# Second layer's experts: rows stored by an indirect scatter in token and choice order, last combination read with plain loads

## The chip, the cores and the metric

One core of one Trainium2 chip runs the whole program in one launch. The metric is device time in microseconds (us): the median of the runs of the kernel before is 1483.16 us (3 runs, 1478.87 to 1484.14).

## The reference, cut to what matters

Two layers of gated attention-like mixing and mixture-of-experts feed-forward work on 2048 tokens of 256 floats (batch 2, sequence 1024). What the change touches is the last part, the experts of the second layer:

```python
scores = sigmoid(x @ gate_w.T)                      # 2048 tokens x 32 experts
_, topk_ids = top_k(scores + e_bias, 4)             # four experts for each token
topk_w = take_along_axis(scores, topk_ids, axis=1)
topk_w = topk_w / sum(topk_w, axis=1, keepdims=True)
...                                                 # out[t] = sum over the 4 experts e of
                                                    #   topk_w * (silu(x w1[e]) * (x w3[e])) w2[e]
x = x + tanh(g_ffn[1]) * out
```

All of it is in float32, and the hidden width of an expert is 192.

## The kernel before, in words

The program is a row of stages. Each stage is a block in which every engine has its own instruction stream; at the end of a block each engine runs a drain instruction and then a barrier holds all engines until the last has arrived (the profile books the drain and the barrier on the line of the `with nc.Block()` or on a line near it). The last three stages are these.

`route` (layer 1) turns the router's scores into tables. Every token has four choices, which makes 8192 rows; they are sorted by expert and padded to tiles of 128 rows, 95 tiles in all (`NT1`). For each of the 95 x 128 places the stage must know which token stands there. It finds this with 64 small matmuls of one-hot matrices, which all add into one PSUM bank; the result is the token number plus one, or zero where a place is padding. VectorE turns it into `token_u`, the list of tokens by tile (lines 821 to 827), and also keeps `slot_u`, the place that each token's k-th choice was given (line 794).

`experts1` runs over the 95 tiles with rings of four buffers. For one tile: VectorE copies one column of `token_u` into `tcol` (line 897); GpSimd starts an indirect gather that fetches the 128 token rows from `xn1` in DRAM (`move_tiles`, line 864); TensorE transposes them (line 1045), multiplies by `w1` and `w3` of the tile's expert (line 1051), transposes the hidden rows (line 1057) and multiplies by `w2` (line 1066); ScalarE does the silu and two copies out of PSUM; VectorE does the product (line 1139) and copies the result to `ysb` (line 1127). SyncE stores `ysb` as a plain tile of 128 rows of 1 KB in tile order into `y1` (line 1156). Tiles overlap: VectorE, in its turn for tile j, copies out tile j-2 and makes the column for tile j+5; TensorE transposes the rows of tile j+2. The program's order on each engine is fixed, with a loop of four tiles per turn (`tile_loop`). The first layer's `experts0` has the same form but stores by an indirect scatter from GpSimd (line 875), into token and choice order, seven calls or so behind the gathers (`LAG`).

`combine` (layer 1) takes 16 tiles of 128 tokens. For each, GpSimd issues four indirect gathers (one for each choice, line 1201) that fetch the rows from `y1` by `slot_u` into a ring of four tiles. VectorE first computes the four weights of each token (lines 1214 to 1222) and then adds the four weighted rows to `x` (line 1233, 64 operations); ScalarE's queue stores each finished tile to the output (line 1247). VectorE and ScalarE run this in loops with register arithmetic. The first layer's combination has no gathers: SyncE loads each tile of 128 tokens with one plain transfer (line 1187).

## Time and profile before

| what | value |
|---|---|
| runs, median (lowest to highest) | 1483.16 us (1478.87 to 1484.14) |
| span of the profiled execution, first to last instruction | 1482.6 us |
| PE, DVE, ACT, POOL busy share of the span | 80%, 51%, 40%, 22% |
| gathers of `experts1` and `experts0` (line 864) | 134 of 952 ns |
| gathers of the last combination (line 1201) | 64 of 971 ns |
| mean DMA rate over the span | 78 GB/s |

The profile gives no time of the profiled execution beyond its span; the span lies 0.6 us under the median of the runs. The engines are PE (TensorE), DVE (VectorE), ACT (ScalarE), POOL (GpSimd) and SP (SyncE). A line with "q" after the engine, as in POOLq, is an instruction of that engine's sequencer (a wait, a register operation, a drain, or the issue of a transfer). All start times are microseconds from the start of the span.

### The profile page before, as it was taken

How to read it: one execution, taken by the hardware profiler on the slowest of the kernel's cores; microseconds unless marked ns; L12 is line 12 of the kernel's file. 1: busy time of each engine (PE TensorE's matmuls, PEld its weight loads, DVE VectorE, ACT ScalarE, POOL GpSimd, SP SyncE). 2: the span in 40 equal slices, each digit the busy share in tenths (PEclk: the TensorE clock that was granted, in tenths of full speed). 3: DMA queues.
4: the chain of work that ended last, by engine and by line, in shares of the span. 5: the costliest groups of instructions: out<-in, count | busy, mean ns of one | idle time of the engine just before them, and what ended most of it. 6: DMA issues, size and time to landing. Idle time of an engine off the chain costs nothing. (4 is left out here: it accounts for less than half of the span.)

```text
span 1482.6 us, 24652 instructions
## 1 busy us (share of the span) xinstructions
PE 1186.0 (80%) x5790; PEld 661.9 (45%) x5792; DVE 751.7 (51%) x2017; ACT 592.7 (40%) x1307; POOL 320.0 (22%) x527
## 2 busy tenths in 40 slices
PE   3485999999992587999999999998717999999200
PEld 1374667677672341233323323323614777777100
DVE  4334333333334467788888878851484333333432
ACT  2342111111110440677767767776425333333000
POOL 2001222222220602010110111100002333333564
PEclk9965999999996795899999999999756999999655
DMA  9710011011012774330330231202801333334343
GB/s 311 282 57 15 27 35 35 28 35 35 28 28 96 232 223 78 38 46 2 46 46 15 31 46 17 29 2 68 213 11 50 102 100 103 99 100 99 91 116 96
DMA packets 86256, 115.39 MB, mean 78 GB/s; under 512 B 14902, under 2 KB 71120, under 8 KB 86058
## 3 DMA queue, kind: packets, MB, share of 16 engines
q1 hardware_dynamic: 69594, 71.24, 19.0%
q0 software_dynamic: 14288, 41.30, 9.7%
q10 hardware_dynamic: 2304, 2.10, 0.4%
q8 instruction: 22, 0.36, 0.1%
q14 instruction: 48, 0.39, 0.1%
HBM read 84.01 MB, written 30.38 MB: 77 GB/s over the span
## 5 line engine op out<-in xcount | busy, mean ns | idle before, releaser
L1868 DVE TENSOR_REDUCE arena<-ps 128x1 f32<-128x512 f32 x512 | 327.9, 682 | 73.8 <-PE ps L1709 66.9
L1839 ACT ACTIVATE arena<-ps 128x512 f32<-128x512 f32 (+1 forms) x576 | 304.4, 598 | 143.0 <-PE ps L1750 141.8
L1750 PE MATMUL ps<-arena 99*128 99x512 bf16 (+1 forms) x576 | 218.0, 391 | 5.9 <-ACT arena L1839 5.6
L864 POOL DMA_INDIRECT xg<-xn,tcol x134 | 127.6, 952 | 433.0 <-DVE tcol L897 431.5
L1709 PE MATMUL ps<-arena 96*128 96x512 bf16 x512 | 207.0, 407 | 13.6 <-DMA arena<-k_parts 11.2
L1739 PE MATMUL ps<-arena 128*17 128x512 f32 (+1 forms) x1152 | 154.2, 607 | 2.1 <-ACT arena L1839 1.0
L967 ACT ACTIVATE scratch<-ps 128x512 f32<-128x512 f32 x78 | 46.6, 598 | 249.8 <-PE ps L942 249.8
L942 PE MATMUL ps<-arena,scratch 128*128 x312 | 142.4, 599 | 0.7 <-ACT scratch L962 0.6
L934 PE MATMUL ps<-arena,scratch 128*128 x624 | 141.2, 379 | 0.7 <-DVE scratch L999 0.7
L1051 PE MATMUL ps<-arena,scratch 128*128 x380 | 140.0, 491 | 0.2 <-issue 0.2
L1750 PEld LDWEIGHTS ps<-arena 99*128 99x128 bf16 (+1 forms) x576 | 57.2, 102 | 180.7 <-ACT arena L1839 138.9
L934 PEld LDWEIGHTS ps<-arena,scratch 128*128 128x128 f32 x624 | 115.6, 190 | 15.5 <-issue 1.4
L984 DVE TENSOR_TENSOR ysb<-ps,arena 128x256 f32<-128x256 f32 x39 | 16.6, 425 | 179.3 <-PE ps L934 179.3
L1139 DVE TENSOR_TENSOR scratch<-ps,scratch 128x192 f32<-128x192 f32 x95 | 34.0, 357 | 131.1 <-ACT scratch L1108 103.1
L1066 PE MATMUL ps<-arena,scratch 96*128 x380 | 97.8, 380 | 0.4 <-DVE ysb L1127 0.4
L999 DVE TENSOR_SCALAR scratch<-ps,arena 128x128 f32<-128x128 f32 x312 | 84.2, 343 | 26.6 <-PE ps L951 26.6
L942 PEld LDWEIGHTS ps<-arena,scratch 128*128 128x128 f32 x312 | 56.9, 193 | 58.4 <-issue 58.4
L1709 PEld LDWEIGHTS ps<-arena 96*128 96x128 bf16 x512 | 51.6, 101 | 62.2 <-DVE arena L1868 25.4
L1051 PEld LDWEIGHTS ps<-arena,scratch 128*128 128x128 f32 x380 | 65.4, 192 | 26.3 <-issue 1.5
L1658 POOL TENSOR_TENSOR scratch<-arena 128x64 f32 (+1 forms) x64 | 18.8, 294 | 265.7 <-DVE arena L1887 251.5
L1201 POOL DMA_INDIRECT arena<-y,slot_u x64 | 62.1, 971 | 40.6 <-issue 19.3
L1066 PEld LDWEIGHTS ps<-arena,scratch 96*128 96x128 f32 x380 | 64.5, 190 | 6.0 <-issue 0.9
(289 smaller groups left out, 1366.1 us busy)
## 6 DMA issues: line engine op xcount, KB each, us to landing
arena<-in_L_ffn_W SPq DMA_DIRECT2D x16, 1024.0 KB, 12.8
y<-ysb SPq DMA_DIRECT2D x95, 128.0 KB
arena<-in_L_ffn_w POOLq DMA_DIRECT2D x26, 384.0 KB, 10.1
arena<-in_L_ffn_w SPq DMA_DIRECT2D x44, 192.0 KB, 6.6
arena<-k_parts SPq DMA_DIRECT2D x48, 137.6 KB, 5.0
arena<-q_parts SPq DMA_DIRECT2D x96, 64.0 KB, 5.0
xn<-scratch SPq DMA_DIRECT2D x32, 128.0 KB, 1.7
scratch<-y SPq DMA_DIRECT2D x16, 256.0 KB, 2.8
```

What stands on the lines that cost most here:

```text
L864: pool.indirect_dma_start(out=e.xg[:, r, :], out_offset=None, in_=e.xn[layer], in_offset=bass.IndirectOffsetOnAxis(ap=e.tcol[:, r:r + 1], ...
L934: last = nc.tensor.matmul(ps[:, YB, 0:D], hT[:, k, :], e.w2[:, ex, k, :], start=(k == 0), stop=(k == HK0 - 1))
L942: ins = nc.tensor.matmul(ps[:, HB0 + n, :], xT[:, k, :], e.w1[:, ex, k, n * HB:(n + 1) * HB], start=(k == 0), stop=(k == DK - 1))
L999: v.tensor_scalar(hT[:, k, :], ps[:, TB + k // HALF, (k % HALF) * P:(k % HALF + 1) * P], e.b1T[:, bass.ds(ex * HK0 + k, 1)], 0.0, ALU.add, ...
L1051: ins = nc.tensor.matmul(ps[:, GB + r % 2, 0:2 * I1], xT[:, r % 2, k, :], e.w13[:, ex, k, :], start=(k == 0), stop=(k == DK - 1))
L1066: last = nc.tensor.matmul(ps[:, YB + r % 2, 0:D], aT[0:IH, r % 2, k, :], e.w2b[0:IH, ex, k, :], start=(k == 0), stop=(k == 1))
L1201: pool.indirect_dma_start(out=yg[:, u, k, :], out_offset=None, in_=e.y[1], in_offset=bass.IndirectOffsetOnAxis(ap=e.slot_u[:, i, k:k + 1], ...
L1709: nc.tensor.matmul(ps[:, MAXB + pos % NMAXB, :], e.q_aug[u][0:QROWS, c, h, t * P:(t + 1) * P], e.k_aug[u][0:QROWS, h, CL + k * HB:CL + (k ...
L1739: ins = nc.tensor.matmul(ps[h * 32:h * 32 + HD + 1, AB, :], e.v_g[u][0:rows, mt, h, :], e.prob[s % 2][0:rows, h, :], start=(mt == 0), stop ...
L1750: nc.tensor.matmul(ps[0:rows, SB + n % NSB, :], e.k_aug[u][0:AROWS, h, k0:k0 + rows], e.q_aug[u][0:AROWS, c, h, :], start=True, stop=True) ...
L1839: nc.scalar.activation(e.prob[s % 2][0:rows, h, :], ps[0:rows, SB + (s * GH + h) % NSB, :], ACT.Exp).then_inc(p_ready, 1)
L1868: v.tensor_reduce(e.mx[:, c, h, t, k:k + 1], ps[:, MAXB + pos % NMAXB, :], AX.X, ALU.max).then_inc(max_done, 1)
```

## The change

Four things change.

1. `route`, layer 1: the 64 matmuls now add into four PSUM banks, one for each choice, so that the choice of each place is known too. VectorE works out of them `row_u`, the destination row 4 x token + choice (or a spare row past the end for padding), in some nine operations more; `slot_u` is gone.
2. `experts1`: the plain store on SyncE is gone. GpSimd issues an indirect scatter per tile into `y1` instead, behind its gathers; VectorE copies one more column per tile (`rcol`). At the end GpSimd waits for the last scatters.
3. The four weights of each token are computed by VectorE at the start of `experts1`, after the first four columns.
4. The last combination has no indirect gathers and no ring: SyncE issues 16 plain loads of 512 KB, each 4 KB in one piece per partition, into 16 separate buffers, with no wait between them. VectorE's 64 operations and ScalarE's 16 stores are the same but written out, without a loop.

```diff
@@ make_env
-    e.slot_u = sb("slot_u", [P, NTILE, K1], U32)
-    e.y = [dram("y0", [NTOK * K0 + P, D]), dram("y1", [NT1 * P, D])]
+    e.y = [dram("y0", [NTOK * K0 + P, D]), dram("y1", [NTOK * K1 + RING1 * P, D])]
@@ route, VectorE, layer 1
-            ch(v.tensor_scalar(row_i, row, -1.0, None, ALU.add))
-            v.tensor_scalar(e.token_u[:, 0:nt].bitcast(I32), row_i, NTOK - 1, None, ALU.bitwise_and)
+                ch(v.tensor_reduce(row, ps[:, RB:RB + kk, 0:nt].rearrange("p k n -> p n k"), AX.X, ALU.add))
+                for k in range(1, kk - 1):
+                    v.tensor_scalar(late[k - 1], ps[:, RB + k, 0:nt], 0.0, float(k), ALU.is_gt, ALU.mult)
+                ch(v.tensor_scalar(row_i, row, -1.0, None, ALU.add))
+                v.tensor_scalar(e.token_u[:, 0:nt].bitcast(I32), row_i, NTOK - 1, None, ALU.bitwise_and)
+                v.scalar_tensor_tensor(none, row, 0.0, flat(spares)[:, 0:nt], ALU.is_equal, ALU.mult)
+                ch(v.tensor_scalar(late[kk - 2], ps[:, RB + kk - 1, 0:nt], 0.0, float(kk - 1), ALU.is_gt, ALU.mult))
+                v.scalar_tensor_tensor(row, row, float(kk), late[0], ALU.mult, ALU.add)
+                ch(v.tensor_tensor(late[1], late[1], late[2], ALU.add))
+                ch(v.scalar_tensor_tensor(none, none, -float(kk), row, ALU.add, ALU.add))
+                v.tensor_tensor(e.row_u[:, 0:nt], none, late[1], ALU.add)
@@ move_tiles
-    LAG = 2 + ring
+    LAG = (2 + ring, 3 + ring)[layer]
...
-            if layer == 1 or (isinstance(j, int) and j < 0):
+            if isinstance(j, int) and j < 0:
                 return
             pool.wait_ge(y_ready, j + 1)
             pool.sem_inc(carrier, 1)
...
+        for r, stored in enumerate(y_stored):
+            pool.wait_ge(stored, 16 * ((nt - 1 - r) // len(y_stored) + 1))
@@ experts1, VectorE
                 if at_least(j, RING1):
                     dve.wait_ge(y_stored[r], turn * 16)
+                v.tensor_copy(e.rcol[:, r:r + 1], e.row_u[:, bass.ds(j, 1)])
                 dve.wait_ge(y_raw, j + 1)
...
+            def weights():
+                ch = Chain(dve, gate_step)
+                for k in range(K1):
+                    ch(v.tensor_tensor(score.rearrange("p (i e) -> p i e", e=E1), e.chosen[:, k], e.sig, ALU.mult))
+                    ch(v.tensor_reduce(e.gate[:, :, k], score.rearrange("p (i e) -> p i e", e=E1), AX.X, ALU.add))
+                ch(v.tensor_reduce(tot, e.gate[:], AX.X, ALU.add))
+                ch(v.reciprocal(tot, tot))
+                ch(v.scalar_tensor_tensor(e.gate[:], e.gate[:], e.tg[:, 3:4], tot..., ALU.mult, ALU.mult))
             for j in range(RING1):
                 token_column(e, dve, j, j, tcol_ready)
+            weights()
             next_column(0, 0)
...
-        @block.sync
-        def _(sp):
-            def body(j, r, turn, first, last):
-                sp.wait_ge(y_ready, j + 1)
-                sp.dma_start(e.y[1][bass.ds(j * P, P), :], e.ysb[:, r, :]).then_inc(y_stored[r], 16)
@@ combine, layer 1
-                for i in range(NTILE):
-                    u = i % U
-                    if i >= U:
-                        pool.wait_ge(added, i - (U - 1))
-                    for k in range(kk):
-                        pool.indirect_dma_start(out=yg[:, u, k, :], out_offset=None, in_=e.y[1], ...)
+            y = e.y[1][0:NTOK * kk, :].rearrange("(i p k) d -> p i k d", k=kk, p=P)
+            for i in range(NTILE):
+                sp.dma_start(yg[:, i, :, :], y[:, i, :, :]).then_inc(got[i], 16)
```

## Rows read from the trace of the kernel before

**Rows 1.** Busy time by stage: window, length, then each engine's, PEclk, DMA share, GB/s.

```profile
1200.00:1300.00 100.00, 100.00 (x464) 71.25 (x464) 32.72 (x117) 38.66 (x117) 36.38 (x39) 1.00 0.33 101
1400.00:1425.00 25.00, 0.00 (x0) 0.00 (x0) 5.76 (x13) 0.00 (x0) 18.55 (x20) 0.50 0.42 121
```

**Rows 2.** Groups of instructions from 1150 us on: busy us, mean ns, idle before.

```profile
L1201 POOL DMA_INDIRECT arena<-y,slot_u x64 | 62.1, 971 | 40.6 <-issue 19.3 <-PEq L1176 17.0 <-DVE x_resident L1233 4.2
L1233 DVE SCALAR_TENSOR_TENSOR x_resident<-arena,gate,x_resident 128x256 f32 x64 | 27.9, 480 | 62.9 <-issue 31.9 <-DMA arena<-y,slot_u 30.4 <-DVE x_resident L1233 0.6
```

**Rows 3.** Timeline where the experts end: start us, length us, what, idle before.

```profile
1380.06 0.42 DVE L1127 COPY ysb<-ps 128x256 f32<-128x256 f32 x1 [0.59 <-PE ps L1066]
1383.79 1.46 POOL L1201 DMA_INDIRECT arena<-y,slot_u  x1 [17.02 <-PEq L1176]
```

**Rows 4.** Timeline of the program's last gather and last additions.

```profile
1468.56 0.95 POOL L1201 DMA_INDIRECT arena<-y,slot_u  x1 [0.31 <-issue]
1474.59 5.23 DVE L1233 SCALAR_TENSOR_TENSOR x_resident<-arena,gate,x_resident 128x256 f32 x13 [0.33 <-DVE x_resident L1233]
```

**Rows 5.** Timeline of the first layer's hand-over from experts to combination.

```profile
455.97 0.43 DVE L984 TENSOR_TENSOR ysb<-ps,arena 128x256 f32<-128x256 f32 x1 [2.27 <-PE ps L934]
457.31 0.97 POOL L875 DMA_INDIRECT y<-ysb,rcol  x1 [4.30 <-DVE ysb L984]
466.59 17.73 SPq L1187 DMA_DIRECT2D scratch<-y  x16
469.76 0.48 DVE L1233 SCALAR_TENSOR_TENSOR x_resident<-scratch,gate,x_resident 128x256 f32 x1 [13.36 <-DMA scratch<-y]
```

**Rows 6.** GpSimd's drains at block ends: ns min/median/max, first and last start us.

```profile
L915 POOLq DRAIN  x1: 6442/6442/6442, 459.9 to 459.9; - x1
L1037 POOLq DRAIN  x1: 8989/8989/8989, 1365.6 to 1365.6; - x1
L1176 POOLq DRAIN  x2: 34/6224/12414, 466.6 to 1462.4; - x2
```

**Rows 7.** Busy time by stage: weight loads at the start, the first layer's combination.

```profile
20.00:30.00 10.00, 5.14 (x16) 2.68 (x16) 1.94 (x9) 4.39 (x16) 0.00 (x0) 1.00 1.04 385
466.00:490.00 24.00, 0.00 (x0) 0.00 (x0) 18.61 (x48) 0.00 (x0) 0.00 (x0) 0.50 0.56 175
```

**Rows 8.** Timeline of the experts' last gather and transpose; a gather until landing (chain).

```profile
1365.83 0.94 POOL L864 DMA_INDIRECT xg<-xn,tcol  x1 [1.65 <-DVE tcol L897]
1372.08 0.38 PE L1045 MATMUL ps<-ident,xg 128*128 128x128 f32 x2
1388.05 2.72 DMA arena<-y,slot_u
```

**Rows 9.** Timeline of GpSimd in the first layer's experts.

```profile
311.19 0.97 POOL L864 DMA_INDIRECT xg<-xn,tcol  x1 [5.72 <-DVE tcol L897]
312.47 0.99 POOL L875 DMA_INDIRECT y<-ysb,rcol  x1 [0.30 <-issue]
```

**Rows 10.** VectorE's token list at the end of routing; a large PSUM reduce (page).

```profile
1123.58 0.25 DVE L824 TENSOR_SCALAR xg<-ps 128x95 int32<-128x95 f32 x1
1123.86 0.21 DVE L827 TENSOR_SCALAR token_u<-xg 128x95 int32<-128x95 int32 x1
L1868 DVE TENSOR_REDUCE arena<-ps 128x1 f32<-128x512 f32 x512 | 327.9, 682 | 73.8 <-PE ps L1709 66.9
```

**Rows 11.** Timeline where the second layer's experts begin.

```profile
1129.38 0.15 DVE L897 COPY tcol<-token_u 128x1 uint32<-128x1 uint32 x1 [4.34 <-PE ps L1045]
1138.38 0.39 PE L1045 MATMUL ps<-ident,xg 128*128 128x128 f32 x2
```

**Rows 12.** The last combination: a piece of the chain, VectorE's and GpSimd's timeline.

```profile
1409.49 0.71 DVEq L1223
...
1420.12 0.48 DVE L1233 SCALAR_TENSOR_TENSOR x_resident<-arena,gate,x_resident 128x256 f32 x1 [2.31 <-issue]
...
1428.59 0.94 POOL L1201 DMA_INDIRECT arena<-y,slot_u  x1 [4.25 <-DVE x_resident L1233]
```

More of the change, by code:

```diff
@@ L674, in route @@
     w = buf([NTILE, kk]); tot = buf([NTILE])
-    row_i = buf([nt]).bitcast(I32); none = buf([nt]) if layer == 0 else None
+    row_i = buf([nt]).bitcast(I32); none = buf([nt])
+    GROUPS = (nt + RING1 - 1) // RING1
+    if layer == 1:
+        spares = buf([GROUPS, RING1]); row = buf([nt]); late = [buf([nt]) for _ in range(kk - 1)]
+    RB = 3
     if layer == 0:
@@ L1150, in _, with combine0 @@
                 out(j, j % RING1, j // RING1)
+def combine0(e):
+    nc, sem = e.nc, e.sem
+    kk = K0
+    U = 4
+    got = [sem(f"co0_got{u}") for u in range(U)]
+    step, added = sem("co0_step"), sem("co0_added")
+    yg = e.carve(0, [U, kk, D], base=e.scr)
+    TURNS = NTILE // U
+    with nc.Block() as block:
         @block.sync
         def _(sp):
-            def body(j, r, turn, first, last):
-                sp.wait_ge(y_ready, j + 1)
-                sp.dma_start(e.y[1][bass.ds(j * P, P), :], e.ysb[:, r, :]).then_inc(y_stored[r], 16)
@@ L1204, in _, with load @@
+            y = e.y[0][0:NTOK * kk, :].rearrange("(k i p) d -> p i k d", k=kk, p=P)
+            def load(t):
+                for u in range(U):
+                    i = t * U + u
+                    if not isinstance(t, int):
+                        sp.wait_ge(added, i - (U - 1))
+                    sp.dma_start(yg[:, u, :, :], y[:, i, :, :]).then_inc(got[u], 16)
+            load(0)
+            with sp.Fori(1, TURNS) as t:
+                load(t)
         @block.vector
@@ new lines, in combine1, with _ @@
+def combine1(e):
+    nc, sem = e.nc, e.sem
+    kk = K1
+    got = [sem(f"co1_got{i}") for i in range(NTILE)]
+    step, added, stored = sem("co1_step"), sem("co1_added"), sem("co1_stored")
+    yg = e.carve(0, [NTILE, kk, D])
+    with nc.Block() as block:
+        @block.sync
+        def _(sp):
+            y = e.y[1][0:NTOK * kk, :].rearrange("(i p k) d -> p i k d", k=kk, p=P)
+            for i in range(NTILE):
+                sp.dma_start(yg[:, i, :, :], y[:, i, :, :]).then_inc(got[i], 16)
+        @block.vector
+        def _(dve):
+            v = nc.vector
+            for pair in range(0, NTILE, 2):
+                for k in range(kk):
+                    for i in (pair, pair + 1):
+                        if k == 0:
+                            dve.wait_ge(got[i], 16)
+                        else:
+                            dve.wait_ge(step, pair * (kk - 1) + (k - 1) * 2 + (i - pair) + 1)
+                        v.scalar_tensor_tensor(e.x[:, i, :], yg[:, i, k, :], e.gate[:, i, k:k + 1], e.x[:, i, :],
+                                               ALU.mult, ALU.add).then_inc(step if k < kk - 1 else added, 1)
+        @block.scalar
+        def _(act):
+            o = e.out.rearrange("b (t p) d -> p (b t) d", p=P)
+            for i in range(NTILE):
+                act.wait_ge(added, i + 1)
+                act.dma_start(o[:, i, :], e.x[:, i, :]).then_inc(stored, 16)
+            act.wait_ge(stored, 16 * NTILE)
```

108 lines of the change are left out of this document (30 added, 78 removed).

## The prediction

> **What bounds the kernel now.** The span is 1482.6 us and the runs' median 1483.16, so I sum against the span and carry the 0.6 us between them. I began with the busy time by stage. While the experts of the second layer run, TensorE is busy for all of the window at full clock [rows 1]; a gather there takes 0.94 us after 1.65 us of waiting for its column [rows 8], and that sum, 2.60 us with the rounding, is the period of one of the 95 tiles. In that stretch GpSimd is 36% busy, DMA moves 101 GB/s: the experts are bound by TensorE and nothing else is near. After them TensorE does nothing; GpSimd is busy 18.6 of 25 us, VectorE 5.8 [rows 1]. The groups by line say what this is: 64 gathers of 0.971 us with 19.3 us of issue gaps (0.31 each), so one every 1.28 us, against 27.9 us of additions [rows 2]. 64 x 1.28 = 82 us. The stage goes from the last copy's end, 1380.48 [rows 3], to 1482.6: 102 us, and its gathers are its bound, with VectorE's waits behind them. The change is about this stage, and the question is what it pays elsewhere: what its work costs on GpSimd in the experts' loop, and at the hand-over.
>
> **Part 1, routing.** Before, the token list took two short operations, 0.25 and 0.21 us [rows 10]. After, it is a reduction over 4 x 95 values and ten operations on 95 values. The 512-value reduce takes 0.68 us [rows 10]; scaled down this is about 0.55. Ten at 0.21 to 0.25 are 2.3 us, less some overlap where no wait stands, plus small waits. 0.55 + 2.3 - 0.46 = 2.4 us; the slot cast that goes takes a little off: **+2.2 us**, all on the path, since the first columns wait for the end of the block. Bounds +1.2 (operations without a wait overlap by half) and +3.5. The matmuls are as many as before, and the spare rows' iota runs on an idle GpSimd.
>
> **Part 2, weights moved.** Eight operations on 512 values, at the 0.68 us of such a reduce [rows 10], and three of about 0.25, in a chain with small gaps: 6.6 us after the first four columns. They are in nobody's way: the fifth column was copied at 1129.38 [rows 11] and would now come some 2.3 us later, while the transpose of its tile is at 1138.38 [rows 11] and a gather lands 2.7 us after its start [rows 8]. **0 us**, at most +1 if the first gathers are held up. In the combination they hid behind gathers; they take nothing out of it.
>
> **Part 3, the experts' loop.** TensorE's work is unchanged. VectorE gains one column copy (0.14 to 0.15 us [rows 11]) in front of a wait for TensorE's result; it is a third busy. SyncE's stores go; the bytes stay. GpSimd now does a gather and a scatter per tile. The first layer's loop has exactly this pair: scatter 1.28 us after gather, then 0.99 and a gap of 0.30, which makes 2.57 us [rows 9]. The period is 2.60. So GpSimd goes from 36% to 99% and keeps up, barely. Behind a late gather stand the next scatter and gather, and TensorE's transpose waits for the gather. There is slack: the last gather starts at 1365.83, is used at 1372.08, and needs 2.7 us [rows 8], so 3.5 us. Over some 87 tiles the pair may grow to 2.60 + 3.5/87 = 2.64 us before TensorE waits at all. **0 us**; the bounds are 0 and the first rival below.
>
> **Part 4, the hand-over.** Before, the last copy ended at 1380.48 and the next stage's first gather began at 1383.79 [rows 3]. Now a scatter must follow and the block must end on GpSimd. The first layer shows it: copy ends 456.40, scatter starts 457.31, and the next stage's first load comes at 466.59 [rows 5], 9.3 us after the scatter's start. Of that, 6.4 us are GpSimd's drain [rows 6], which ended 8.1 us after the scatter's own end. The same drain in the second layer began at 1365.6 and took 9.0 us [rows 6], until 1374.6: hidden under the experts' last tiles because GpSimd had nothing to do there. The change brings it into the open. 1380.48 + 0.91, plus 0.25 because the scatter before it is still running, is 1381.65; + 9.28 gives the first load at **1390.9**. Lower bound: the drain at the program's end ended 1474.8, 5.3 us after the last gather's end [rows 4, 6], which would save 2.8 us. I take the first layer's, since it is the same instruction before the same kind of barrier.
>
> **Part 5, the combination.** First layer: first load to first addition, 3.17 us with 256 KB loads [rows 5]. The wide weight loads moved 385 GB/s at a full DMA share [rows 7]; I take 380, so 524 KB last 1.38 us, 0.7 more than half as much: first addition at 1394.8. The other 15 loads take 20.7 us, and 12 output tiles of 131 KB get in between: 4.1 us. Last landing 1419.6; then seven additions. Thirteen back to back took 5.23 us, 0.402 each [rows 4], so 2.8: last addition ends at 1422.4. VectorE alone would end at 1394.8 + 1.4 + 63 x 0.402 = 1421.5, so both limits nearly meet. The last addition before ended at 1479.82, the span 2.8 us later [rows 4]; now 1425.2. Bounds: 1.9 less (VectorE alone, no late load); at 312 GB/s (175 at a share of 0.56 [rows 7]), 10.5 MB take 6 us more.
>
> **Sum.** 1425.2 + 2.2 = 1427.4 for the span, 55.2 less than before; with 0.6 for the median: **1428 us**. Its own range is 1420 to 1436.
>
> **Rivals.**
> *GpSimd becomes the bound of the experts' loop.* For: 99% load, and two copies per tile on VectorE between two places in SBUF. If each of the two (0.15 us) held GpSimd up for its length, the pair is 2.57 + 0.30 = 2.87 us, and 87 x 0.27 - 3.5 = 20 us are lost: 1448. Against: the first layer's pair stands in a loop with the same two copies and is 2.57, though there they seldom meet. On this the Trainium skill, "SBUF — State Buffer", section "Who interferes with whom", speaks against the change: copies with input and output in SBUF can take a port pair that GpSimd needs for writing descriptors, and the loser waits for the whole instruction. By that rule the time is this rival's; the trace's gathers of 0.94 us next to VectorE's work [rows 8] don't show it.
>
> *VectorE's issue slows down under dense GpSimd traffic: slower than before.* Inside the last combination VectorE's operations stand 2.8 us apart in places, with "issue" before them and no releaser [rows 12], where back to back they take 0.40. It set in at 1409.5, where a sequencer instruction of VectorE suddenly takes 0.71 us [rows 12], 26 us after the first of the gathers that ran without a pause [rows 3], and GpSimd's pause of 4.25 us up to 1428.59 [rows 12] is where it goes. The experts' loop would now have that density for some 220 us. If it sets in each 26 us, that is eight times; four VectorE operations per tile at 2.8 are 11.2 us instead of 2.6, and one such tile starves GpSimd and so ends it: 8 x 8.6 = 69 us, 1497 us. It decides from seven slow tiles on (55/8.6). Against: it struck in a loop with register arithmetic between operations; the experts' loop has that too, but one stage in one trace is little.
>
> *The loads run slow* (16 in flight with stores between, first layer's average of 175 GB/s as it stands): 10.5 MB take 60 instead of 28 us, 1460. Against: there VectorE set the pace.
>
> *It does less than it says* (loads wait for something I don't see, a hand-over twice as long): within 1% of before. Nothing speaks for it.
>
> **Chances.** Forecast 0.72, GpSimd as bound 0.13 (up to 1448), slow loads 0.04, slow issue 0.09, little change 0.02. The range 1419 to 1450 holds the first and nearly all of the second. A measurement here tells 0.5% from no change. Faster by more: 0.72 + 0.13 + 0.04, and 0.89 it is; slow issue is slower mostly, 0.08; within 0.5%, 0.03.
>
> **What would show it.** The profile after should have no GpSimd work past about 1384 us; GpSimd at 95% or more in the experts' loop with TensorE's period still 2.60; a drain of 6.4 us on GpSimd right after the last scatter landed; first load near 1393 (with routing's 2.2); 16 loads in about 28 us and additions in pairs waiting on loads only lightly. I am wrong if TensorE waits on gathers in the loop, if VectorE's "issue" gaps appear there, or if the drain is short.

## The result, and the profile after

Run in turns with the kernel before on one chip, the changed kernel takes 1491.5 us (median of 6 runs, 1488.55 to 1496.89) against 1483.65 us before (6 runs, 1478.87 to 1485.09): a ratio of 1.0059, 95% interval 1.0035 to 1.0082. It is slower by 0.6% where 1428 us were forecast. Its profiled span is 1495.2 us. The experiments below add the half of the answer that this first result hides: on another chip the same kernel takes 1431 us.

First, busy time by stage in the changed kernel, with the same columns as [rows 1]. The first line is the window of the experts' loop that stands there, the second the new last combination.

```profile
1200.00:1300.00 100.00, 87.78 (x349) 57.98 (x348) 25.95 (x117) 28.90 (x89) 57.33 (x59) 0.91 0.24 76
1460.00:1485.00 25.00, 0.00 (x0) 0.00 (x0) 17.99 (x46) 0.00 (x0) 0.00 (x0) 0.50 0.86 338
```

TensorE was busy for all of this window and is now busy for 87.8 us of it, with 349 matmuls instead of 464. GpSimd, which should be at 99% of the time counting its gaps, is busy 57 us. So it is not GpSimd that sets the pace. The length of the loop is taken here, and in every run below, from the start of the last of the first tile's four gate and up matmuls to the start of the last of the last tile's. Before, this took 242.8 us (1132.88 to 1375.65), after it takes 310.3 us (1136.60 to 1446.92): the loop lost 67.6 us. The period of a tile is still 2.60 us in the median, but 34 of the 94 periods are over 3 us, the longest 8.0; before, none was over 2.61. Below, a loop that loses time in this way is said to stall.

The changed kernel's engines at one of the longer ones, in the timeline (start, length, what, idle time before and what ended it):

```profile
1171.56 0.97 POOL L883 DMA_INDIRECT xg<-xn,tcol  x1 [0.30 <-issue]
1172.24 1.55 PE L1073 MATMUL ps<-arena,scratch 128*128 x4 [0.81 <-issue]
...
1172.84 0.99 POOL L894 DMA_INDIRECT y<-ysb,rcol  x1 [0.30 <-issue]
1175.28 0.33 ACT L1130 ACTIVATE scratch<-ps 128x192 f32<-128x192 f32 x1 [3.17 <-PE ps L1073]
1175.50 0.37 ACT L1124 ACTIVATE scratch<-ps 96x256 f32<-96x256 f32 x1
1175.64 0.36 DVE L1162 TENSOR_TENSOR scratch<-ps,scratch 128x192 f32<-128x192 f32 x1 [5.57 <-ACT scratch L1130]
...
1177.12 2.07 PE L1088 MATMUL ps<-arena,scratch 96*128 x4 [0.64 <-ACT scratch L1124]
1177.23 0.97 POOL L883 DMA_INDIRECT xg<-xn,tcol  x1 [3.40 <-DVE tcol L916]
```

The silu on ScalarE waits for the product that ended at 1173.8 and starts at 1175.28, 1.5 us later, with nothing between; VectorE waits for the silu; TensorE's four 96-row products stretch to 2.07 us, where they took 1.03 before; and GpSimd, whose two DMAs had stood 1.28 us apart, waits 3.40 us for a column from VectorE. Each engine looks late because of another. In other places it is TensorE's own issue or VectorE's that is late. The timeline of GpSimd alone shows the rhythm, here at the loop's start:

```profile
1144.11 0.95 POOL L883 DMA_INDIRECT xg<-xn,tcol  x1 [1.57 <-DVE tcol L916]
1145.37 1.00 POOL L894 DMA_INDIRECT y<-ysb,rcol  x1 [0.30 <-issue]
...
1150.59 0.99 POOL L894 DMA_INDIRECT y<-ysb,rcol  x1 [0.30 <-issue]
1153.98 0.97 POOL L883 DMA_INDIRECT xg<-xn,tcol  x1 [2.40 <-DVE tcol L916]
...
1160.40 0.99 POOL L894 DMA_INDIRECT y<-ysb,rcol  x1 [0.30 <-issue]
1163.84 0.97 POOL L883 DMA_INDIRECT xg<-xn,tcol  x1 [2.45 <-DVE tcol L916]
```

Six DMAs 1.28 us apart, then 3.4 us from one start to the next, then six again. Between 1140 and 1440 us there are 31 such gaps of over 2 us, and the stretch between two of them most often holds six DMAs. Six in 5 x 1.28 + 3.4 = 9.8 us are 0.61 a us; the window above has 59 in 100 us.

The hand-over and the combination went as forecast. Timeline of the changed kernel, and its drain from the list of line 1059 (the answers to [rows 3] and [rows 6]):

```profile
1451.25 0.42 DVE L1150 COPY ysb<-ps 128x256 f32<-128x256 f32 x1 [0.52 <-PE ps L1088]
...
1452.74 0.97 POOL L894 DMA_INDIRECT y<-ysb,rcol  x1 [0.30 <-issue]
1462.65 7.51 SPq L1247 DMA_DIRECT2D arena<-y  x15
1466.22 0.48 DVE L1259 SCALAR_TENSOR_TENSOR x_resident<-arena,gate,x_resident 128x256 f32<-128x256 f32 x1 [14.54 <-DMA arena<-y]
1467.49 25.02 DVE L1259 SCALAR_TENSOR_TENSOR x_resident<-arena,gate,x_resident 128x256 f32<-128x256 f32 x63 [0.79 <-DMA arena<-y]
```

```profile
L1059 POOLq DRAIN  x1: 6919/6919/6919, 1455.5 to 1455.5; - x1
```

From the last copy's end (1451.67) to the end of the span are 43.5 us, against 102.1 before. The balance of the two spans: +3.7 up to the start of the loop (2.1 of it the longer token list, the rest was late before the list began), +67.6 in the loop, -58.6 behind it, together 12.7, and the spans differ by 12.6.

### The profile page after: what moved, and what is told of

Its sections match the earlier page's. It is cut to its first block and busy times, and to the rows that moved or that the text cites. A ratio compares the mean times of both kernels' runs of the same rounds, so it can differ in the third digit from the quotient of the medians.

```text
span 1495.2 us, 24340 instructions
## 1 busy us (share of the span) xinstructions
PE 1216.0 (81%) x5791; PEld 672.0 (45%) x5792; DVE 756.4 (51%) x2120; ACT 590.8 (40%) x1307; POOL 355.5 (24%) x559
## 5 line engine op out<-in xcount | busy, mean ns | idle before, releaser
L1073 PE MATMUL ps<-arena,scratch 128*128 x380 | 151.9, 525 | 8.6 <-issue 5.6
L894 POOL DMA_INDIRECT y<-ysb,rcol x134 | 132.8, 991 | 73.7 <-issue 35.6
L961 PE MATMUL ps<-arena,scratch 128*128 x312 | 142.8, 601 | 0.7 <-ACT scratch L981 0.6
L953 PE MATMUL ps<-arena,scratch 128*128 x624 | 141.2, 379 | 0.7 <-DVE scratch L1018 0.7
L953 PEld LDWEIGHTS ps<-arena,scratch 128*128 128x128 f32 x624 | 115.6, 190 | 15.5 <-issue 1.4
L1088 PE MATMUL ps<-arena,scratch 96*128 x380 | 105.3, 401 | 12.4 <-DVE ysb L1150 6.5
L1073 PEld LDWEIGHTS ps<-arena,scratch 128*128 128x128 f32 x380 | 69.1, 202 | 42.2 <-issue 18.1
L961 PEld LDWEIGHTS ps<-arena,scratch 128*128 128x128 f32 x312 | 57.1, 193 | 58.6 <-issue 58.6
L1088 PEld LDWEIGHTS ps<-arena,scratch 96*128 96x128 f32 x380 | 68.4, 201 | 23.6 <-issue 17.3
## 6 DMA issues: line engine op xcount, KB each, us to landing
arena<-in_L_ffn_W SPq DMA_DIRECT2D x16, 1024.0 KB, 12.7
```

The costliest lines, as they stand in the source:

```text
L894: pool.indirect_dma_start(out=e.y[layer], out_offset=bass.IndirectOffsetOnAxis(ap=e.rcol[:, r:r + 1], axis=0), in_=e.ysb[:, r, :], in_offs ...
L953: last = nc.tensor.matmul(ps[:, YB, 0:D], hT[:, k, :], e.w2[:, ex, k, :], start=(k == 0), stop=(k == HK0 - 1))
L961: ins = nc.tensor.matmul(ps[:, HB0 + n, :], xT[:, k, :], e.w1[:, ex, k, n * HB:(n + 1) * HB], start=(k == 0), stop=(k == DK - 1))
L1073: ins = nc.tensor.matmul(ps[:, GB + r % 2, 0:2 * I1], xT[:, r % 2, k, :], e.w13[:, ex, k, :], start=(k == 0), stop=(k == DK - 1))
L1088: last = nc.tensor.matmul(ps[:, YB + r % 2, 0:D], aT[0:IH, r % 2, k, :], e.w2b[0:IH, ex, k, :], start=(k == 0), stop=(k == 1))
```

## The experiments

The kernels ran in seven groups, each on one chip beside the kernel before. This matters more than was thought at first, so the chip's number stands with each group. No chip was used for two groups.

### Which part stalls: chip 0

**Stores on SyncE again**, in tile order, gathers alone on GpSimd:

```diff
 def scatter(j, r):
-    if isinstance(j, int) and j < 0:
+    if layer == 1 or (isinstance(j, int) and j < 0):
         return
+@block.sync                      # in experts1, as before the change
+    sp.wait_ge(y_ready, j + 1)
+    sp.dma_start(e.y[1][bass.ds(j * P, P), :], e.ysb[:, r, :])...
```

> The changed kernel with the scatters of the experts' loop undone alone: SyncE stores each tile in tile order, as before, and GpSimd only gathers; routing, row columns, moved weights and the wide loads of the combination stay. It leaves out the right order of the rows (the combination reads rows of the wrong tokens). Theory A (density: two DMAs per 2.6 us tile that GpSimd issues hold up the other engines): the loop loses none of its 67.3 us and GpSimd's drain is hidden again under the last tiles, so the first load comes some 3.3 us after the last copy instead of 11.0: 1491.5 - 67.3 - 7.7 = 1417 us. Rival B (the random-row write itself is slow): also 1417. Rival C (the added row column copy on VectorE, or something of routing, stops the engines): the stalls stay, 1484 us.

Measured, near the 1417 of theories A and B: 1418.7 us, the kernel before 1474.95; ratio 0.9627 (0.9595 to 0.9659). The loop takes 242.4 us.

**Scatters alone**, gathers for the first four tiles only:

```diff
 def gather(j, r):
+    if layer == 1 and not (isinstance(j, int) and j < ring):
+        return
```

> The changed kernel with its scatters, but with gathers for the first four tiles only (every later tile computes on the rows of those four, so gathered input is left out). GpSimd issues one indirect DMA per tile, a scatter. Theory A (density): no stall, first to last gate and up product 242.8 us as before the change, the drain still exposed: 1491.5 - 67.3 = 1424 us. Rival B (random-row writes slow the engines): the stalls stay, 310 us for the loop, 1490 us. Between them, half the loss, would say both count.

Measured: 1428.3 us, ratio 0.9692 (0.9662 to 0.9723); loop 243.7 us.

**The kernel before with two gathers per tile:**

```diff
 def scatter(j, r, turn=None):
+    if layer == 1:
+        pool.wait_ge(extra[(r - 2) % ring], ...)
+        pool.indirect_dma_start(out=spare[:, r % 2, :], out_offset=None, in_=e.xn[1],
+            in_offset=bass.IndirectOffsetOnAxis(ap=e.token_u[:, r:r + 1], axis=0)).then_inc(extra[r], 16)
+        return
```

> The kernel before with a second gather per tile in the experts' loop, at the place of the scatter, into two spare buffers that nobody reads (the stores stay on SyncE, the combination stays with 64 gathers). Theory A (density, whatever the two are): about 67 us are lost in the loop and some 7 at its end, where the drain is no longer hidden: 1483.7 + 74 = 1558 us, within 30. Rival B (random-row writes): 1484 to 1491 us, the period stays 2.60.

Measured, 76 us under theory A's 1558: 1482.4 us, ratio 1.0053 (1.0036 to 1.0070); loop 242.3 us, no period over 2.61. Of the 7 us that it is slower, some 6 stand at the loop's end: GpSimd's drain, 6.93 us long here, is no longer hidden, and the first gather of the combination starts 9.4 us after the last copy's end, where it was 3.3 in the profile of the prediction.

**Plain stores by GpSimd** in place of the scatters:

```diff
+if layer == 1:
+    pool.dma_start(e.y[1][bass.ds(j * P, P), :], e.ysb[:, r, :]).then_inc(y_stored[r], 16)
+    return
 pool.indirect_dma_start(out=e.y[layer], out_offset=...e.rcol...
```

> The changed kernel with each scatter replaced by a plain store in tile order that GpSimd issues (order of the rows left out, bytes and queue kept). Theory A as density of any DMA of GpSimd: the stalls stay, 1480 to 1500 us. Theory A', only indirect DMAs count: the loop takes 242.8 us, 1424 us or a little less. Rival B (random rows written): also 1424. So it tells A from A', and with the run of two gathers A' from B.

Measured: 1428.5 us, ratio 0.9686 (0.9658 to 0.9714); loop 242.1 us.

None of the four loops is more than 0.9 us longer than the 242.8 of the kernel before. Read alone, these four say that two gathers are harmless, a scatter is harmless, and only the two together hurt. That reading was wrong, and the flaw is that the group held no stalling kernel as its control.

### The control, and the column copy: chip 3

**The changed kernel unchanged:**

> The changed kernel once more, beside the three runs that follow, because the kernel before read 1475 us in the last runs and 1484 us in the first. If the stalls belong to the kernel, its loop again takes some 310 us between the first and the last gate and up product and the time is 1480 to 1500 us. If they come and go with the chip, the loop takes about 243 us and the time is about 1425 us.

Measured: 1489.0 us, the kernel before 1482.87; ratio 1.0051 (1.0029 to 1.0073); loop 305.8 us.

**No row column copy**: the scatters use the row columns of the first four tiles in turn (in the first layer `rcol` stays):

```diff
-    v.tensor_copy(e.rcol[:, r:r + 1], e.row_u[:, bass.ds(j, 1)])
-    out_offset=bass.IndirectOffsetOnAxis(ap=e.rcol[:, r:r + 1], axis=0)
+    out_offset=bass.IndirectOffsetOnAxis(ap=(e.rcol if layer == 0 else e.row_u)[:, r:r + 1], axis=0)
```

> The changed kernel without VectorE's copy of the row column in the second layer's loop: each scatter takes the row columns of tiles 0 to 3 in turn, four fixed columns of scattered rows (so the rows of the later tiles are left out, and the combination loads rows of the first layer's results instead, with the same bytes). Theory D (the mix: gathers and scatters to scattered rows in one dense stream of GpSimd hold up the other engines): the stalls stay, the loop takes 280 us or more. Rival E (two VectorE copies per tile between places in SBUF, under a GpSimd that never pauses, are what holds the engines up): no stalls, 243 us, 1424 us for the whole.

Measured: 1492.2 us, ratio 1.0056 (1.0037 to 1.0076); loop 307.2 us.

**The same with rows 0 to 511 in order** (the index columns made once by `iota`):

> As the run with fixed scattered rows, but the four fixed columns hold rows 0 to 511 in order, so that each indirect scatter writes 128 neighbouring rows. Theory D, if scattered addresses matter: no stalls, 243 us in the loop. Theory D, if it is the indirect write beside the indirect read whatever the rows: stalls stay, 280 us or more. Rival E: no stalls in either of the two.

Measured: 1491.3 us, ratio 1.0058 (1.0041 to 1.0076); loop 309.8 us. The stalls need neither the added copy nor scattered addresses.

**Two gathers per tile and a second column copy**, in the kernel before:

```diff
+    v.tensor_copy(e.rcol[:, r:r + 1], e.token_u[:, bass.ds(j, 1)])
     dve.wait_ge(y_raw, j + 1)
     v.tensor_copy(e.ysb...
```

> The kernel before with two gathers per tile, which lost nothing in its loop, and in addition the second column copy per tile on VectorE. Theory D (gather and scatter mixed): no stalls, loop 242.5 us, 1475 to 1485 us as without the copy. Rival E (second copy under dense GpSimd): stalls as in the changed kernel, loop 280 us or more, some 1520 to 1550 us.

Measured: 1554.0 us, ratio 1.0493 (1.0433 to 1.0553); loop 314.4 us. No scatter is in this loop, so the scatter is not needed either. Two things had changed against the run with two gathers that lost nothing: a 0.14 us copy, and the chip.

### The chip: chip 2

> The first four experiments and the next four ran on two different chips (the kernel before: 1475 us on the one, 1483 us on the other), and every run that stalled was on the second. So the changed kernel is put beside two of the first four and one of the next four on one chip. Theory F (the stalls depend on the chip): where the kernel before reads about 1475 us, the changed kernel's loop takes 243 us and its time is about 1425 us; where it reads about 1483, 306 to 310 us and 1490. Theory G (they depend on the kernel alone): 306 to 310 us and 1480 to 1490 us on either.

> The kernel before with a second gather per tile once more. Theory A with F (density, on a chip that stalls at all): it stalls wherever the changed kernel of the same four runs stalls, loop 300 to 315 us and about 1550 us, and does not where that one does not (1482 us). Rival E with G (the second column copy on VectorE decides): it never stalls, loop 242.5 us, 1480 to 1492 us.

> The same with the second column copy on VectorE, once more. Theory A with F: as the run without the copy on this chip, 1482 us if the chip does not stall, 1550 us if it does. Rival E with G: 1554 us as the last time, 70 us more than without the copy.

> The changed kernel with plain GpSimd stores in place of the scatters once more (order of the rows left out). GpSimd works for 1.55 of 2.60 us here instead of 1.96. Theory A with F: if density decides, this is below the point and stays at 243 us and about 1428 to 1436 us even where the changed kernel stalls; if it stalls there too (above 260 us in the loop), any two DMAs per tile are enough.

Measured, with the kernel before at 1475.2 us: the changed kernel **1430.9 us** (4 runs, 1426.80 to 1432.54), ratio 0.9680 (0.9656 to 0.9705), loop 243.4 us; two gathers 1481.2, ratio 1.0027 (1.0010 to 1.0044); with the copy 1481.5, ratio 1.0036 (1.0022 to 1.0050), loop 242.5 us against 314.4 on chip 3; plain stores 1428.4, ratio 0.9668 (0.9642 to 0.9693). Theory F fits and theory G falls: one and the same kernel stalls in a group on one chip and not in a group on another. Since no chip was used twice, whatever else differed between two groups goes with the chip here. Busy time in one window, first the changed kernel on chip 2, then the run with two gathers and the copy on chip 2, then that run on chip 3:

```profile
1200.00:1300.00 100.00, 100.00 (x464) 71.14 (x463) 34.55 (x153) 38.74 (x116) 73.40 (x75) 1.00 0.31 98
```

```profile
1200.00:1300.00 100.00, 100.00 (x464) 71.32 (x463) 34.61 (x153) 38.59 (x116) 71.85 (x77) 1.00 0.54 150
```

```profile
1200.00:1300.00 100.00, 86.75 (x361) 57.39 (x360) 26.07 (x120) 28.92 (x90) 55.77 (x59) 0.97 0.40 117
```

Where nothing stalls GpSimd issues 0.75 to 0.77 indirect DMAs a us, and the second row does it at 150 GB/s, so those bytes alone do not make a loop stall; where it stalls it issues 0.59. The granted clock is 0.97 of full speed on average in the stalling window here and 0.91 in that of the changed kernel, with TensorE busy for 86.8 and 87.8 of 100 us; on chip 2, with TensorE busy throughout, it is 1.00. In the trace of the changed kernel on chip 2, GpSimd's DMAs run 106 in a row with no gap of 2 us:

```profile
1157.35 0.99 POOL L894 DMA_INDIRECT y<-ysb,rcol  x1 [0.31 <-issue]
1158.68 0.97 POOL L883 DMA_INDIRECT xg<-xn,tcol  x1 [0.34 <-issue]
1159.95 0.99 POOL L894 DMA_INDIRECT y<-ysb,rcol  x1 [0.30 <-issue]
1161.27 0.97 POOL L883 DMA_INDIRECT xg<-xn,tcol  x1 [0.33 <-issue]
```

### The drain taken off the path: chip 8

**One block.** The last combination moves into the experts' block; SyncE waits for the scatters themselves:

```diff
 # experts1, sync
+for r in range(RING1):
+    sp.wait_ge(y_stored[r], 16 * ((NT1 - 1 - r) // RING1 + 1))
+for i in range(NTILE):
+    sp.dma_start(yg[:, i, :, :], y[:, i, :, :]).then_inc(got[i], 16)
 # VectorE's additions and ScalarE's stores follow in the same block
```

> The changed kernel with the last combination moved into the experts' block: SyncE waits for the scatters' own semaphores and issues the 16 loads at once, VectorE and ScalarE go on into the additions and stores, and nobody waits for GpSimd's 6.9 us drain. Nothing is left out. Theory: the drain was 7.2 us of the path (from the last scatter's landing at 1390.7 to the first load at 1398 in the run that did not stall), so 7 us less on any chip: 1424 us on a chip that does not stall, 1483 us on one that does, which there is no gain over the kernel before. Rival (the loads or the additions run slower beside the drain): less than 3 us gained.

Measured: **1421.9 us** (4 runs, 1421.46 to 1425.20), the kernel before 1475.62; ratio 0.9640 (0.9602 to 0.9682). The timeline:

```profile
1384.06 0.42 DVE L1158 COPY ysb<-ps 128x256 f32<-128x256 f32 x1 [0.53 <-PE ps L1091]
...
1385.54 0.97 POOL L894 DMA_INDIRECT y<-ysb,rcol  x1 [0.30 <-issue]
1388.10 4.94 SPq L1209 DMA_DIRECT2D arena<-y  x10
```

```profile
L1062 POOLq DRAIN  x1: 6919/6919/6919, 1388.3 to 1388.3; - x1
```

In the timeline and the list of line 1062, the drain is as long as in the changed kernel (6.92 us) and starts 0.2 us after the first load, with nobody behind it. From the last copy's end (1384.48) to the first load are 3.6 us instead of 10.9 on chip 2; the forecast of 7 us holds. This is the fastest correct version; it was timed beside the kernel before alone, so that it also beats the changed kernel rests on the 7.3 us between the two traces, not on runs in turns.

**Half of the scatters**, SyncE storing the other tiles:

```diff
-    if isinstance(j, int) and j < 0:
+    if isinstance(j, int) and j < 0 or layer == 1 and r % 2:
```

> The changed kernel with a scatter for every second tile, while SyncE stores the others in tile order behind them (right order of those rows left out, and the combination loads the first layer's rows, the same bytes). GpSimd works 1.46 of 2.60 us instead of 1.96. On a chip that does not stall: 243 us in the loop, about 1428 us. On one that stalls, theory A with F (density decides): none or under 10 us lost, loop 243 to 253 us, about 1430 to 1440 us. Rival H (stalls come with each scatter beside gathers): half of the loss, loop 275 us, 1460 us.

**Plain stores once more:**

> The changed kernel with plain GpSimd stores in place of the scatters, a third time (order of the rows left out), for a chip that stalls. GpSimd works 1.55 of 2.60 us. Chip that does not stall: 1428 us again. Chip that stalls, theory A with F: as the run with half of the scatters, under 10 us lost in the loop. Rival I (any second DMA of GpSimd per tile is enough): loop 300 us, 1485 us.

Measured: 1424.4 us, ratio 0.9644 (0.9606 to 0.9682), and 1425.0 us, ratio 0.9672 (0.9625 to 0.9719), with loops of 243.1 and 242.6 us. The kernel before at 1475.6 already tells that this chip does not stall, so both say nothing of how dense a stalling loop has to be. One thing in the run with half of the scatters differs: GpSimd's drain behind them takes 2.9 us and not 6.9, and from the last copy's end to the end of the span are 39.5 us instead of 43.4 on chip 2.

```profile
L1059 POOLq DRAIN  x1: 2925/2925/2925, 1391.0 to 1391.0; - x1
```

### Three densities in one loop: chip 13

Since the chip cannot be chosen, the control went into the kernel:

```diff
+if part == 2 or part == 1 and r % 2:
+    pool.dma_start(e.y[1][bass.ds(... + j * P, P), :], e.ysb[:, r, :]).then_inc(y_stored[r], 16)
+    return
-with pool.Fori(0, turns) as t:
+for t0, t1, part in ((0, 7, 0), (7, 14, 1), (14, turns, 2)):
+    with pool.Fori(t0, t1) as t:
```

> One kernel with three densities of GpSimd's DMAs in one loop, for a chip that stalls. Changed kernel, but tiles 0 to 32 are scattered as they are (GpSimd works 1.96 of 2.60 us per tile), of tiles 33 to 60 every second is stored plainly in tile order by GpSimd and the others scattered (1.75), and tiles 61 to 94 are all stored plainly (1.55); the right order of the plainly stored rows is left out, and the combination loads the first layer's rows, the same bytes. On a chip that does not stall: 243 us in the loop, 1428 us. On one that does, theory A with F (density decides, with a point between): 20 to 25 us lost in the first third, 0 to 15 in the second, under 3 in the last, 1450 to 1465 us. Rival I (any second DMA per tile is enough): about 22 us lost in each third, 1490 us. The first third is the control in the same trace.

Measured: 1450.0 us, the kernel before 1481.45; ratio 0.9800 (0.9770 to 0.9830); loop 266.6 us. Lost against 2.597 us a tile: 21.5 us over the first 34 tiles, 1.3 over the next 28, nothing over the last 32; the changed kernel on chip 3 lost 17.9, 20.2 and 23.6 over the same tiles. The 1.3 us of the middle part fall in its first four tiles. Busy time of the three parts:

```profile
1155.00:1235.00 80.00, 69.28 (x286) 45.92 (x284) 20.42 (x92) 22.12 (x70) 46.98 (x48) 0.96 0.25 80
1258.00:1310.00 52.00, 52.00 (x242) 37.03 (x241) 17.95 (x80) 20.15 (x61) 34.47 (x40) 1.00 0.30 96
1320.00:1385.00 65.00, 65.00 (x302) 46.29 (x301) 22.61 (x100) 25.17 (x76) 39.38 (x51) 1.00 0.36 102
```

GpSimd's groups in the middle part:

```profile
L883 POOL DMA_INDIRECT xg<-xn,tcol x20 | 19.3, 967 | 15.4 <-DVE tcol L921 10.6 <-issue 3.5 <-DVE ysb L1155 1.4
L897 POOL DMA_INDIRECT y<-ysb,rcol x10 | 10.0, 998 | 3.1 <-issue 2.4 <-DVE tcol L921 0.6
L895 POOL DMA_DIRECT2D y<-ysb x10 | 5.9, 589 | 0.0
```

TensorE is busy for 52 of 52 us beside 40 DMAs of GpSimd, 30 of them indirect: 0.77 DMAs a us, but 0.58 indirect ones. The first part, which stalls, has 48 indirect ones in 80 us, 0.60. So the stalls come with the density of the indirect DMAs on such a chip, and "any second DMA" falls. What this run shows of the limit: 0.58 a us does not stall and the 0.77 that the kernel wants does. The next run adds a point between them.

### Pauses instead of fewer DMAs: chip 7

```diff
+for _ in range(pauses[u]):       # (0,1,0,1), then (1,1,1,1), then (0,0,0,4) per four tiles
+    pool.wait_ge(paused, ...)
+    pool.sem_inc(carrier, 1)
+    e.nc.gpsimd.memset(e.small[:], 0.0).then_inc(paused, 1)
```

> The run with one block, with pauses for GpSimd's DMAs in the experts' loop: after some of its DMAs GpSimd fills a small unused buffer, 0.21 us each. Tiles up to about 36 (counted by the gather): one such pause in every second tile; up to about 64: one in each tile; after that four together in every fourth. Nothing is left out. GpSimd's work per four tiles grows from 10.28 to about 10.8, 11.3 and 11.3 us against TensorE's 10.39. On a chip that does not stall, that costs about 3, 7 and 5 us, less the 3.5 us of slack: 1422 + 12 = 1434 us. On one that stalls, theory J (a stall sets in where GpSimd's DMAs run without a pause; a tenth of the time is enough, as in the middle third of the last run): stalls go in the second part and perhaps the others, loop 243 + 12 to 270 us, 1435 to 1460 us. Rival K (it is DMAs per time over a longer stretch, and a fill is no pause): the loop stays above 300 us, 1480 to 1490 us.

Measured: 1483.8 us (10 runs), the kernel before 1484.63; ratio 1.0000 (0.9983 to 1.0018); loop 303.1 us. By the total rival K held, and theory J missed; but part of the total is the fills' own. In the last part eight DMAs stand together and then four fills:

```profile
1368.36 0.20 POOL L916 MEMSET small<- 128x128 f32 x1 [0.15 <-POOL small L916]
1369.42 0.97 POOL L883 DMA_INDIRECT xg<-xn,tcol  x1 [0.85 <-issue]
...
1378.40 0.99 POOL L894 DMA_INDIRECT y<-ysb,rcol  x1 [0.30 <-issue]
1379.39 0.22 POOL L916 MEMSET small<- 128x128 f32 x1
...
1381.54 0.98 POOL L883 DMA_INDIRECT xg<-xn,tcol  x1 [0.85 <-issue]
```

Eight in 12.1 us are 0.66 a us, and that part lost 15.5 us over 24 tiles. Its windows, for the three patterns:

```profile
1155.00:1235.00 80.00, 66.25 (x279) 43.88 (x278) 20.88 (x94) 22.49 (x70) 49.44 (x60) 0.98 0.25 80
1250.00:1320.00 70.00, 60.40 (x256) 40.21 (x255) 19.37 (x88) 21.41 (x66) 44.59 (x61) 0.98 0.24 76
1335.00:1405.00 70.00, 61.79 (x268) 41.01 (x267) 19.00 (x86) 20.79 (x64) 46.79 (x62) 1.00 0.29 81
```

Less the fills (12, 20 and 18 of them) these are 48, 41 and 44 indirect DMAs, 0.60, 0.59 and 0.63 a us. The first two patterns leave GpSimd nearly as dense as it was, and their tiles lose 19.2 us (the first 34) and 22.1 us (the next 28), about as much as in the changed kernel.

The last pattern does not say the same. The turn of four tiles shown above, in which GpSimd waits for nobody, takes 12.12 us, where 11.3 were expected and TensorE needs 10.39. So GpSimd itself is the bound there, at 0.66 DMAs a us, and six such turns lose some 10 us (an estimate from these two rows) without any stall. That leaves about 5 of the 15.5 us for stalls, where the changed kernel lost 14.0 us over these 24 tiles on chip 3 and 20.7 on the chip of the result. At 0.66 indirect DMAs a us the stalls are fewer, and not gone: GpSimd still waits 2.4 us for a column twice in that part.

### Rows or bytes: chip 12

Tiles 33 to 60 scatter rows of half the width, tiles 61 to 94 the first 64 rows of each tile.

> One loop in three parts again, as in the run with three densities, the first part (tiles 0 to 32) the changed kernel's own scatter of 128 rows of 1 KB as the control. Tiles 33 to 60: each scatter writes 128 rows of half the width; tiles 61 to 94: each scatter writes the first 64 rows of full width (the rest of the results is left out, and the combination loads the first layer's rows). On a chip that stalls: if each indirect DMA counts whatever it moves, 20 us are lost in each part, as in the changed kernel; if rows count, 20 us in the second and under 3 in the last; if bytes count, under 3 in both. In all of the runs that stalled GpSimd issued 0.60 to 0.63 indirect DMAs per us over the loop, 190 in 303 to 314 us, and the middle part of the run with three densities, which did not stall, 0.58. On a chip that does not stall: 243 us in the loop and about 1428 us, and only the scatters' own durations are learned.

Measured: 1429.6 us, the kernel before 1476.38; ratio 0.9676 (0.9658 to 0.9694); loop 244.2 us. The chip does not stall, so the question stays open. GpSimd's groups show only its own cost for a scatter: the width does not change it and the number of rows changes it little.

```profile
L900 POOL DMA_INDIRECT y<-ysb,rcol x34 | 30.8, 905 | 16.3 <-issue 8.0 <-DVE ysb L1161 7.4 <-DVE tcol L927 0.9
L903 POOL DMA_INDIRECT y<-ysb,rcol x31 | 30.7, 989 | 9.4 <-issue 9.4
L896 POOL DMA_INDIRECT y_half<-ysb,rcol x28 | 27.6, 987 | 8.5 <-issue 8.5
```

64 rows take 0.905 us, 128 rows 0.989, 128 rows of half width 0.987.

### The chips, side by side

| chip | kernel before, us | changed kernel, us | a loop with two dense indirect DMAs |
|---|---|---|---|
| of the first result | 1483.65 | 1491.5 | stalls, 310 us |
| 3 | 1482.87 | 1489.0 | stalls, 306 us |
| 7 | 1484.63 | (with pauses) | stalls, 303 us |
| 13 | 1481.45 | (first third) | stalls |
| 0 | 1474.95 | not run | two gathers: no, 242 us |
| 2 | 1475.2 | 1430.9 | no, 243 us |
| 8 | 1475.62 | 1421.9 (one block) | no, 244 us |
| 12 | 1476.38 | not run | no, 244 us |

The kernel before belongs to the same two groups: 1475 to 1476.4 us where nothing stalls, 1481 to 1485 us where something does. It has one dense stretch, its last combination. In the traces with two gathers, which keep that combination, the 64 gathers start over 79.7 and 80.2 us on chip 2, 80.8 on chip 0 and 87.7 on chip 3; in the profile of the prediction it was 84.8. VectorE's slow sequencer instructions of [rows 12], 0.69 to 0.74 us each, stand 20 times in the 84.8 and 7 times in the 87.7, and not once in the other three.

The traces differ in one thing more, and it shows before any loop stalls. A DMA moves its semaphore on by 16 steps (624 are recorded for the first layer's 39 scatters, in every trace). In the twelve traces of chips 0, 2, 8 and 12 at most 1.7% of all these steps are not recorded; in the eight of the first result's chip and chips 3, 7 and 13 it is 18 to 32%, the kernel before included. Steps are missing already from the first layer's gathers, whose loop takes the same 320 to 321 us in all twenty traces. So in these traces the two kinds can be told apart from the first layer alone; why the steps are missing is not known.

## Why the prediction was wrong

**What failed is one step, part 3**, "the experts' loop ... 0 us". Its reasoning on GpSimd was right: a pair costs it 2.57 us (0.97 and 0.99 of work and two gaps of 0.30), it keeps up, and where nothing stalls the loop takes 243.4 us, 0.6 more than before. Wrong was that the pair's density was costed by GpSimd's time alone, and that the loop's path was taken to go on through TensorE undisturbed. On the chip of the result the dense pair makes the other engines late, and that costs 67.6 us.

**The rival was there, priced at 69 us and 1497 us, and given 0.09.** The price is near, 67.6 and 1491.5, but by luck: it was built as eight onsets of 8.6 us, one each 26 us, on VectorE. The trace has some 31 episodes of about 2.2 us, one each 10 us, and they hit ScalarE and TensorE as well. The case made against it, "one stage in one trace is little", was weak: the trace held two stretches with a dense stream of GpSimd. In one, the pair of [rows 9], TensorE's tiles were so long that GpSimd then waited 5.7 us; so it was not dense. The only stretch that was, the gathers of the last combination, did show the slow instructions, 26 us after it began [rows 12]. One sighting in one possible place is not little. Two gathers per tile on chips 2 and 3 (loops of 242.3 to 242.5 and of 314.4 us) show that gathers alone, like those of the last combination, are enough for it on such a chip. On a chip that does not stall the same stretch shows none of them, so the rival deserved a larger chance and still no certainty.

**The first rival, GpSimd's own rate,** did not occur: a gather stays at 0.97 us and a scatter at 0.99 with gaps of 0.30, stalling or not, with two column copies per tile on VectorE; the rival had put the pair at 2.87. In the changed kernel on chip 2, between 1150 and 1370 us, the 61 gathers that a column copy falls into take 969 ns and the 23 others 969; of the scatters 64 take 989 ns beside a copy and 20 take 989 without one. The Trainium skill, "SBUF — State Buffer", section "Who interferes with whom", says that a copy within SBUF can take the port pair that VectorE shares with GpSimd, and that the other then waits for the whole instruction. For these copies of one column the trace does not show it. The run without the row copy (307.2 us) and that with it on a chip that does not stall (242.5 us) speak against it as the cause of the stalls.

**Part 1, routing, +2.2 us:** right. From the first operation on the found rows to the end of the last cast before took 0.82 us (1123.58 to 1124.40), after 2.92 (1125.20 to 1128.12): +2.1. The reduction over four banks is 0.54 us long (0.55 forecast):

```profile
1125.20 0.54 DVE L832 TENSOR_REDUCE ysb<-ps 128x95 f32<-128x380 f32 x1
...
1127.68 0.26 DVE L842 TENSOR_TENSOR row_u<-xg,ysb 128x95 uint32<-128x95 f32 x1
1127.85 0.27 DVE L844 CAST expert<-ps 1x128 int32<-1x128 f32 x1
```

**Part 2, the weights, 0 us:** right. They take 6.6 us (1128.68 to 1135.3), as forecast, and from the first gather (1129.46) to the start of the loop (1136.60) are 7.1 us, as before.

**Part 4, the hand-over:** the last copy's end to the first load was forecast at 10.4 us, of which 6.4 drain; it is 11.0 us, of which 6.9 drain, and 10.95 on chip 2. The size is off by 0.6 us and the wait is the one forecast; the run with one block shows that all but 3.6 us of it could have been had back.

**Part 5, the combination:** 34.3 us from first load to the end forecast, 32.5 measured on both chips. The additions alone are the bound: 63 in 25.02 us, 0.397 each; loads and stores together moved 338 GB/s, and from the second addition on the 63 stand back to back. So of the two limits that "nearly meet", the lower one held. What lies behind the last copy was forecast 57.4 us shorter and became 58.6 shorter.

**Where nothing stalls the sum holds:** 1428 forecast, 1430.9 measured. Against the forecast span of 1427.4 the span of 1430.7 on chip 2 has +4.0 up to the start of the loop (the stages before the change ended later in that run), +0.6 in the loop, +0.5 at the hand-over and -1.8 in the combination. The gain there is 44 us, not 55, mostly because the kernel before is itself 8 us faster on such a chip.

**What stays open:** what in such a chip or its setting makes it stall, and whether it is a lasting property of the chip at all, since each was used for one group at one time; whether the recording of the trace takes part, since every execution here was recorded and the stalling chips are the ones whose records are incomplete; which of a DMA's parts counts (its rows, its descriptors, its instruction); and why the engines other than GpSimd are the ones that stop. The traces show late starts after a finished releaser and slow sequencer instructions, but no resource. That the half scatters and the plain stores as whole kernels are fast on a stalling chip was not run; the three parts suggest it. Nor was the kernel with one block: less its 7.3 us it would take 1482 to 1484 us there (an estimate), no clear gain on the kernel before, and the run with pauses, which contains it, gives 1483.8.

## What to carry to other kernels

A step that makes an engine's queue dense is not free because the engine keeps up: look for a stretch of the trace where it is already that dense, and give what the others do there real weight in the forecast, however short it is. Time such a change on several chips before judging it, and put the control into the same kernel or beside it; the four runs of chip 0 made a clean, wrong story. Where a block ends behind GpSimd's DMAs, let the next stage wait for their semaphores instead of the block's end: it gave back 7 us between two traces here.

## What the runs showed of the hardware that was not expected

- One program took two clearly different times in groups on different chips of one type: numbers 3, 7 and 13 stalled (the first result's chip too, whose number is not known) and 0, 2, 8 and 12 did not. The same changed kernel takes 1489.0 to 1491.5 us in the one case and 1430.9 in the other, while within a group it repeats within 0.6%. Each chip was used for one group alone.
- On a stalling chip the loops of six different kernels settle at 0.59 to 0.63 indirect DMAs of GpSimd a us, with gathers or scatters, ordered or scattered rows, 76 or 117 GB/s, with or without fills between (the 0.63 is the part in which the fills alone hold GpSimd to 0.66); a loop with 0.58 indirect and 0.19 plain ones a us stalls no more, and one that GpSimd itself holds to 0.66 still does, less often. These two points come from two chips, 13 and 7.
- A plain store of 128 rows of 1 KB costs GpSimd 0.587 us, an indirect one 0.99, one of 64 rows 0.905.
- GpSimd's drain behind the experts' last DMAs took 6.92 to 6.93 us in 16 of the 20 traces, whether the chip stalls or not. It is no constant: 8.99 us in the kernel before [rows 6] and in the run with stores on SyncE, 8.15 with scatters alone, 2.93 with half of the scatters. The first layer's took 6.44.
